# Second layer's down weights load behind the first layer's last gate product; first block loads ahead of the key numbers; two turns ahead of the last count

## The reference, cut to what matters

```
x = x + _L0_ffn_ref(_L0_cond_ref(x, itok_B_1_198, L0_cond_weights), L0_ffn_W1, L0_ffn_W2, L0_ffn_W3)
x = x + _L1_ffn_ref(_L1_cond_ref(x, ...), L1_ffn_gate, L1_ffn_gate_up_proj, L1_ffn_down_proj)

# _L0_ffn_ref
up_gate = jnp.einsum('bsd,hd->bsh', x, W1)
up_lin = jnp.einsum('bsd,hd->bsh', x, W3)
hidden = fwht(jax.nn.silu(up_gate) * up_lin)
out = jnp.einsum('bsh,dh->bsd', hidden, W2)

# _L1_ffn_ref: 32 experts, 4 of them for each token, inner width 96
router_logits = jnp.einsum('TD,DE->TE', x, gate)
top_k_weights, top_k_indices = jax.lax.top_k(jax.nn.softmax(router_logits), 4)   # then scaled to sum 1
gate_up = jnp.einsum('TD,EDF->TEF', x, gate_up_proj)
g, u = jnp.split(gate_up, 2, axis=-1)
next_states = jnp.einsum('TEF,EFD->TED', u * jax.nn.silu(g), down_proj)
next_states = (next_states * router_weights[..., None]).sum(axis=1)
```

## Time and profile before

| | |
|---|---|
| timed runs, median (lowest to highest of 3) | 968.32 us (965.82 to 968.96) |
| profiled execution, span | 1005.7 us |
| profiled execution, its own time | not given beside the span |
| TensorE busy in the span | 854.8 us, 85% |
| VectorE, ScalarE, GpSimd busy | 563.5, 346.7, 384.1 us |
| chain that ended last | PE 57%, DVE 14%, issue 10%, DMA 9% |

### The profile page before, as it was taken

One profiled execution on the slowest core, in us unless ns is written; L12 is line 12 of the kernel. 1 busy time (PEld: TensorE's weight loads), 2 busy tenths in 40 slices (PEclk: granted clock), 3 DMA queues, 4 the chain that ended last, 5 costly groups with the idle time before them and its releaser, 6 DMA issues.

```text
span 1005.7 us, 16540 instructions
## 1 busy us (share of the span) xinstructions
PE 854.8 (85%) x5239; PEld 683.1 (68%) x5239; DVE 563.5 (56%) x1659; ACT 346.7 (34%) x1007; POOL 384.1 (38%) x405
## 2 busy tenths in 40 slices
PE   2999998946888899687468999979987989999997
PEld 1787776725776777576367788877445756777786
DVE  5547888543565566357657999561533443444243
ACT  3334352512232233111246888502423232222221
POOL 7200628264555556675645541000165002334100
PEclk9999999977999999899668999969977998999999
DMA  9244203788866433453678878000522102332222
GB/s 353 46 157 95 75 18 106 288 186 230 232 174 202 127 101 99 152 201 100 130 162 169 182 171 242 8 1 1 176 83 94 59 6 72 107 99 73 85 66 102
DMA packets 68179, 126.43 MB, mean 126 GB/s; under 512 B 20224, under 2 KB 50265, under 8 KB 65455
## 3 DMA queue, kind: packets, MB, share of 16 engines
q1 hardware_dynamic: 46783, 75.49, 25.1%
q0 software_dynamic: 20800, 47.76, 17.1%
q10 hardware_dynamic: 512, 2.13, 1.0%
HBM read 87.39 MB, written 43.30 MB: 130 GB/s over the span
## 4 chain that ended last, share of the span: by engine, by line
PE 57%; DVE 14%; issue 10%; DMA 9%; ACT 4%; POOL 3%; another core or an unknown queue 2%; SPq 1%; ACTq 0%; DVEq 0%; POOLq 0%
PE ps L470 17%; PE ps L807 10%; PE ps L838 6%; PE ps L817 3%; DMA big<-mid 2%; DVE early L1969 2%; PE ps L828 2%; DVE work L1963 1%; PE ps L2558 1%; POOL sent_d L909 1%; PE ps L2409 1%; PE ps L2513 1%; PE ps L2276 1%; PE ps L2452 1%
## 5 line engine op out<-in xcount | busy, mean ns | idle before, releaser
L909 POOL DMA_INDIRECT sent_d<-mid,slot_i x88 | 98.3, 1117 | 120.6 <-DVE mid L629 68.2
L851 ACT ACTIVATE early<-ps 128x256 f32<-128x256 f32 x134 | 51.4, 383 | 208.2 <-PE ps L817 164.3
L869 DVE TENSOR_TENSOR early<-early,ps 128x96 f32<-128x96 f32 (+1 forms) x134 | 37.2, 278 | 123.1 <-ACT early L857 67.3
L807 PE MATMUL ps<-big,early 128*128 x380 | 85.9, 350 | 19.7 <-DVE early L869 13.9
L900 POOL DMA_INDIRECT back_d<-early,mid x78 | 79.0, 1013 | 58.5 <-DVE early L883 37.2
L838 PE MATMUL ps<-early 96*128 (+1 forms) x346 | 99.6, 389 | 1.1 <-DVE early L883 0.9
L807 PEld LDWEIGHTS ps<-big,early 128*128 128x128 f32 x380 | 68.2, 201 | 35.9 <-issue 32.1
L504 DVE TENSOR_TENSOR hidl<-work,hidh 128x512 fp32r<-128x512 f32 (+1 forms) x56 | 38.7, 691 | 84.4 <-ACT hidh L497 80.2
L900 POOL DMA_INDIRECT back_d<-big,mid x39 | 38.4, 984 | 119.6 <-DVE big L883 113.7
L510 ACT ACTIVATE work<-ps 128x512 f32<-128x512 f32 (+1 forms) x56 | 33.3, 595 | 138.6 <-PE ps L470 132.5
L807 PE MATMUL ps<-early 128*128 x156 | 56.2, 484 | 4.6 <-ACT early L851 4.4
(11 more groups left out here) (440 smaller groups left out, 2103.6 us busy)
## 6 DMA issues: line engine op xcount, KB each, us to landing
mid<-sent_d SPq DMA_DIRECT2D x117, 130.0 KB
big<-back_d SPq DMA_DIRECT2D x8, 512.0 KB
mid<-back_d SPq DMA_DIRECT2D x8, 512.0 KB, 6.2
early<-back_d SPq DMA_DIRECT2D x16, 256.0 KB, 3.2
early<-in_w SPq DMA_DIRECT2D x3, 1024.0 KB, 11.7
big<-in_gate SPq DMA_DIRECT2D x1, 3072.0 KB
big<-in_up SPq DMA_DIRECT2D x1, 3072.0 KB
early<-in_gu SPq DMA_DIRECT2D x1, 2816.0 KB, 10.4
```

What stands on the lines that cost most here:

```text
L807: last = nc.tensor.matmul(ps[:, 2 + j % 2, 0:2 * F].rearrange("p (g n) -> p g n", g=2), L.yTb[j % len(L.yTb)][:, k * P:(k + 1) * P], L.gu[ ...
L851: nc.scalar.activation(L.yTb[b % ring_y], ps[:, b % 2, 0:2 * P], ACT.Copy).then_inc(s["turn_sb"], 1)
L869: nc.vector.tensor_tensor(L.hb[j % ring_h], L.sgb[j % 2], ps[:, 2 + j % 2, F:2 * F], ALU.mult)\
L909: nc.gpsimd.indirect_dma_start(out=sent_d, out_offset=bass.IndirectOffsetOnAxis(ap=L.slot_i[:, i:i + 1], axis=0), in_=L.rows[c][:, t, n, : ...
```

## The change

It has four parts, all around the end of the first layer.

- The first layer's weights lie elsewhere in `early`: high parts of gate and up in words 4096 to 8191, down weights in 8192 to 12287. Words 0 to 8191 are then free when the last gate product is done.
- SyncE's wait before the six loads of `l1_down` is for the 32nd count of `gu_ready` (the last gate and up product of the first layer) in place of `acc_used`. The spare filler and the key numbers are no longer issued around them, but behind the first four block loads.
- TensorE does turns 0 and 1 of the block loop between the last two counts.
- ScalarE copies tiles 2 and 3 of the last chunk right after their logits, ahead of the last share, in place of inside its block loop.

```diff
-        l0_down = early[:, 4096:6144].rearrange("p (m n) -> p m n", n=D)
-        w2mix = early[:, 6144:8192].rearrange("p (c n) -> p c n", n=D)
+        l0_down = early[:, 8192:10240].rearrange("p (m n) -> p m n", n=D)
+        w2mix = early[:, 10240:12288].rearrange("p (c n) -> p c n", n=D)
...
-        l0_high = rounded("l0_high", "early", 8192, [4096])
+        l0_high = rounded("l0_high", "early", 4096, [4096])
...
-        l0_down2 = [rounded("l0_downh", "early", 4096, [M0, D]), rounded("l0_downl", "early", 6144, [M0, D])]
+        l0_down2 = [rounded("l0_downh", "early", 8192, [M0, D]), rounded("l0_downl", "early", 10240, [M0, D])]
...
             sp.dma_start(l1_up, a["up1"]).then_inc(s["big1"], 16)
-            sp.wait_ge(s["fill_set"], 2)
-            sp.dma_start(sent_d[SPARE1:SPARE1 + P, :].rearrange("(q r) n -> q (r n)", r=FILL), filler[0:P // FILL, :])\
-                .then_inc(s["cond"], 16)
-            sp.wait_ge(s["acc_used"], NCH)
+            sp.wait_ge(s["gu_ready"], NCH * M0)
             for q in range(4):
...
-            sp.wait_ge(s["rows_ps"], NT)
-            k0 = first_at["key"][0]
-            assert first_at["keyless"][0] == k0 + WK
-            sp.dma_start(zm[:, 0:2 * WK], a["first"][:, k0:k0 + 2 * WK]).then_inc(s["keys"], 16)
             sp.wait_ge(s["tables"], 2)
...
                 sp_block(sp, L1, b, starts)
-                if b == 2:
+                if b == AHEAD - 1:
+                    sp.wait_ge(s["rows_ps"], NT)
+                    k0 = first_at["key"][0]
+                    assert first_at["keyless"][0] == k0 + WK
+                    sp.dma_start(zm[:, 0:2 * WK], a["first"][:, k0:k0 + 2 * WK]).then_inc(s["keys"], 16)
+                    sp.wait_ge(s["fill_set"], 2)
+                    sp.dma_start(sent_d[SPARE1:SPARE1 + P, :].rearrange("(q r) n -> q (r n)", r=FILL),
+                                 filler[0:P // FILL, :]).then_inc(s["cond"], 16)
                     sp.wait_ge(s["tables"], L1.table0 + AT_FILLS)
-                    sp.wait_ge(s["fill_set"], 2)
...
                 act_logits(act, NCH - 1, t)
+            for t in (2, 3):
+                act_copies(act, NCH - 1, t)
             act_share(act, L1, NCH)
             nc.scalar.activation(warm[:, 1:2], C["ones"][:, 0:1], ACT.Silu)
             for b in range(NBK + L1.lag):
                 act_block(act, L1, b)
-                if b in (0, 1):
-                    act_copies(act, NCH - 1, 2 + b)
...
             pe_count(pe, L1, NCH - 1)
+            owners = {}
+            for b in range(L1.lag):
+                pe_block(pe, L1, b, owners)
             pe_count(pe, L1, NCH)
 
             pe.wait_ge(s["tables"], 2)
             pe.wait_ge(s["big1"], 32)
             pe.wait_ge(s["slots_ready"], NCH + 1)
             pe.wait_ge(s["rows_sb"], NT - 2)
-            owners = {}
-            for b in range(NBK + 3 * L1.lag):
+            for b in range(L1.lag, NBK + 3 * L1.lag):
```

## The result

| | before | with the change |
|---|---|---|
| timed runs, median (lowest to highest) | 968.41 us (962.48 to 972.28, 20 runs) | 962.75 us (956.88 to 969.01, 20 runs) |
| ratio, with its 95% interval | | 0.9943 (0.9924 to 0.9961) |
| profiled execution, span | 1005.7 us | 955.3 us |

The change takes 5.7 us off, between 3.8 and 7.4 by the interval. The 50 us between the two spans are no gain: the execution profiled for `before` was itself a long one. In it ScalarE waited 43.9 us in all, up to 8.7 us at a time, for releasers that the trace does not know ("remote"; the earlier trace rows has one).

A forecast was written before the change was run, and what follows sets the result against it. Transfers queued at the seam between first layer and second layer's experts, some 10 us, were taken as the bound. VectorE's first product moving from 235.07 to 227.4 gave -7.7 us: 998.0 span, 960.6 time; range 953.0 to 966.5.

The forecast's parts named there:

- Down weights from 195.3: SyncE's six down-weight loads were to issue behind the last gate product, from 195.3 to 201.6, 6.32 us as before.
- Rival E: At SyncE's queue: the six loads go no earlier, held by an earlier wait, so nothing moves; no chance of its own.
- The last send, S = 217.0: Chunk 2's last GpSimd send was to land at 217.0, with 214.9 and 220.06 as ends.
- my worst end: At the seam: last send at 220.06, loads of 5.62 us, first product at 233.1; gain 2.0, time 966.3.
- Block load 3.0 us, count 1.6 later, keys at 223.4: At the seam: block 0 lands at 220.8, the count ends at 222.1 instead of 220.5, keys land at 223.4.
- VectorE's chain is late next: After the keys, VectorE's second-table operations take 4.0 us; its first product moves from 235.07 to 227.4, by 7.7 us.
- Copies ahead of the share: ScalarE's early copies let the second half of sends follow at 229.3 and end at 239.2, 4.6 us earlier.
- 37.4 us less than the span: The timed median, 968.32, against the profiled span, 1005.7; the change in microseconds was subtracted from the median without scaling.
- rival A: Behind the seam: stalls of TensorE go too, 5.8 us on top, 13.5 in all, 954.8; chance 0.19.
- B: At chunk 2's sends: they stay late, sharing DMA engines with the weights; gain 2.0 to 5, middle 964.8; chance 0.14.
- C: In the fills after the seam: DMA traffic takes the gain back, 3 us at 225 GB/s; 967 at most; chance 0.09.
- D: At GpSimd: the weights hold up its send descriptors, the seam ends 7.4 us later, time 975.7; chance 0.06.

## Why the prediction was right, and where it wasn't

The forecast was 7.7 us off 968.32; 5.7 came, and 962.75 lies within its range. The mechanism came as described: the weights went in the quiet stretch, the last send and block 0 landed sooner, and VectorE's chain was late next. Step by step:

- **Down weights from 195.3**: 195.71, six issues in 4.53 us instead of 6.32. Right, since the change moves the filler too. What was missed is what had held the weights. I looked at the space in the buffer and the wait for the last sum, and took the spare filler for "one issue, 0.36 us". The filler's issue at 208.53 stood in the timeline, 0.4 us ahead of the first down load, and the list of waits had it with 29.5 us. A kernel with nothing but the filler moved has a seam of 34.2 against 33.3 to 34.0. Rival E, loads held by an earlier wait, was given no chance: by that list it would have come true had the filler stayed ahead, but no kernel with the early wait and the filler ahead was run.
- **The last send, S = 217.0**: 212.73 + 3.14 = 215.87, near the best end, 214.9. The bytes were counted as one queue with the sends at its end, but the send found the engines partly free: 0.66 busy from 209 to 218. The sharing between queues that the Trainium skill describes ("DMA: Bandwidth & Descriptors", queues, rings and completion order) is what the other kernels show: with the weights issued 10.2 us after the first send the last one took 6.46 and 6.55 us, with 15.9 it took 7.27, with 2.6 it took 3.14. The trace agrees with that rule: in the third profile of the change the two sends issued ahead of the weights took 2.5 us each, the next two 5.4 and 7.8, the last 2.9. That it would speak against this change was my worst end, and it did not come to that: the weights stood in the queues 17 us ahead of that send.
- **Block load 3.0 us, count 1.6 later, keys at 223.4**: block 0 was used 2.2 us after issue, at 218.86. The count waited 2.0 us for the transposes, near the 1.6 of the sum, but its input was there at 218.07 and not at 220.25, so that the ends table came at 222.23 (224.0 in the sum). The keys were issued at 218.62, 1.8 us ahead of the sum, and took 4.0 us instead of 3.0; they came just behind the table, at 222.65 or so.
- **VectorE's chain is late next**: right. From its first operation at 222.69 to the first product at 226.92 are 4.2 us (4.0 in the sum), and the product came 0.5 us earlier than the 227.4 forecast. That this was so near is in part luck. The chain stands behind the ends table in VectorE's list as well as behind the keys, and the sum started it with the keys at 223.4 although its own ends table was only at 224.0; by its own terms the product was at 228.0 or later, a gain of 7.1 at most. The count's input, 2.2 us earlier than assumed, made up for it.
- **Copies ahead of the share**: the second half starts at 227.36 (229.3) and the sends end at 237.3 (239.2). But the term was put down to the wrong part: without the moved copies they end at the same time (44.1). What frees them is block 0's landing.
- **The size**. Against before's second profile the seam is 6.5 to 7.3 us shorter in the three profiles of the change, turn 33 comes 6.7 to 9.0 us earlier, and the time falls by 5.7; the forecast's 7.7 lies just outside the interval of 3.8 to 7.4. From turn 33 to the end before took 675.3 us, the three of the change 676.5 to 679.0, the others 674.6 to 681.9. Whether a microsecond or more is given back later in the program no run here tells.
- **"37.4 us less than the span"**: the difference is right, but I took the stalls in that span for those of a usual execution. Where both are known, the span is some 2 us below that execution's own time (955.3 and 957.4). It did no harm to the sum, since that was subtracted, but it did to rival A: its stall of 4.34 us in the earlier trace rows was of that one execution, and the second profile has none there. What is true in A is small: from first product to turn 33 it takes 51.9 to 53.9 us where before took 54.0. One sign that I had named against the forecast did show: later block loads still took over 6 us (6.88 at 227.11, 6.60 at 245.19). The second profile of before had 8.10 and 6.76 in that stretch, so this did not touch the gain at the seam.
- **Rivals.** B, that sends stay late, fits the kernels with weights at 10.2 and not the change. C, that the fills take it back, is not seen in the three profiles of the change, which are not longer there than before; the kernel with the table's operations moved shows the same mechanism for a further gain of 1 to 2 us. D fell: each send kept GpSimd 0.97 to 1.03 us beside the weights.

```profile
194.45 1.03 POOL L909 DMA_INDIRECT sent_d<-mid,slot_i  x1 [0.30 <-issue]
...
212.73 0.97 POOL L909 DMA_INDIRECT sent_d<-mid,slot_i  x1 [0.30 <-issue]
```

So the gain divides like this. Moving the spare filler and its wait behind the down weights: 6.4 us of seam. Loading the weights 7.6 us earlier still, for which the buffers had to be moved: 1.4 more at the seam where the count's input comes at the same 26.3 (34.2 to 32.8), which the times (961.5 beside 957.2, but ratios of 0.9943 and 0.9931 with intervals that overlap) don't settle. Blocks ahead of keys, turns ahead of the count, copies ahead of the share: no gain that can be measured, with up to 2 us of waiting of the count in the change's profiles by the turns.

## What to carry to other kernels

Before a transfer is made able to start earlier, ask which wait ahead of it in its own queue is met last: here the list of waits named a filler that nobody needed for another thirty blocks, and moving that one issue gave, as far as the times can tell, what all four parts gave. A big load that goes wholly ahead frees the small urgent transfer (3.14 us instead of 7.3 to 7.8); what remains of the gain is set by the next chain (here a table of small operations, then the loads themselves), so take each part away by itself before keeping it. And a work item moved ahead of a small urgent one should be sure to be ready first: where it wasn't, the count waited 5.4 us behind it.

## What the runs showed of the hardware

- One execution in a profile can be 4% longer than the kernel's timed runs (1005.7 against 968.3 us) at nearly the usual granted clock (0.921, and 0.939 in the second profile), with 43.9 us of waits of ScalarE, up to 8.7 us each, whose releaser the trace does not know; that they are the whole loss was not shown. A second profile is worth having before small stalls are priced.
- A scatter of 128 rows took the longer, the later direct loads on another queue were issued ahead of it: 3.14, 6.5 and 7.3 us with 3.1 MB issued 17, 9 and 4 us ahead, 7.8 us with 1.4 us (the third profile of the change), 2.5 us ahead of them. A direct load of 128 rows in the same queue as the weights was in use 9.0 us after issue when it was issued 11.7 us behind their first, and 2.9 us after issue when 16.9 us behind.
- The DMA engines' busy share does not tell how much they move. From 226 to 276 it was 0.87 to 0.91 at 229 to 248 GB/s in every kernel but the first profile of before (0.85, 230). From 209 to 226 it was 1.04 with 295 GB/s in the kernel with the filler behind, 0.97 with 288 in the one with the weights late again, and 1.05 with 225 in the first profile of before, each with weights in flight. No run here shows what makes that difference.
